# Graph attention layer on one core: row scales turned as 48 columns and spread through memory, with another order of the VectorE work

## The reference

```
q, k = x @ Wq.T, x @ Wk.T            v = x @ Wv.T + bv
scores = q k^T / sqrt(384) + 2*adj          per head, 128 x 128
row_nonzero = any(scores != 0)              per row and head
scores = where(row_nonzero, scores, -inf)
p = nan_to_num(softmax(scores))
out = (p v) @ Wo.T + bo
result = layernorm(x + out)
```

## Time and profile before

| | |
|---|---|
| time, median of 3 runs | 660.97 us (660.78 to 662.17) |
| profiled execution, its own time | 661.33 us |
| its span | 659.5 us |
| busy share of PE, DVE, ACT, POOL | 97%, 76%, 78%, 62% |
| granted clock of TensorE | 0.999 |
| transfers | 45.88 MB, mean 70 GB/s |

### The profile page before, as it was taken

How to read it: one execution, slowest core, us unless ns; L and a number is a source line. 1 busy time by engine, 2 the same in 40 slices (tenths; PEclk the granted TensorE clock), 3 DMA queues, 4 the chain that set the end, 5 groups by cost and what they waited for, 6 DMA issues and landing times.

```text
span 659.5 us, 18322 instructions
## 1 busy us (share of the span) xinstructions
PE 638.3 (97%) x6060; PEld 550.3 (83%) x6060; DVE 502.6 (76%) x2319; ACT 517.6 (78%) x1942; POOL 410.4 (62%) x500
## 2 busy tenths in 40 slices
PE   9999999999999999999999999999999999999774
PEld 5788888888888888888888888888888888888673
DVE  4667887877887777887877887777877877877884
ACT  5678887878878788877878878788877878877782
POOL 1557665756756666765766856666765756845662
PEclk9999999999999999999999999999999999999999
DMA  9300312121121210212121131210212111011111
GB/s 306 122 4 9 106 57 105 57 74 44 48 105 58 104 50 19 95 59 104 58 86 41 38 106 58 104 50 29 85 58 105 57 50 36 32 58 58 49 49 49
DMA packets 17951, 45.88 MB, mean 70 GB/s; under 512 B 1984, under 2 KB 7104, under 8 KB 17856
## 3 DMA queue, kind: packets, MB, share of 16 engines
q1 hardware_dynamic: 17424, 44.11, 19.3%
q10 hardware_dynamic: 432, 0.59, 0.3%
HBM read 32.11 MB, written 12.58 MB: 68 GB/s over the span
## 4 chain that ended last, share of the span: by engine, by line
PE 67%; POOL 16%; issue 8%; DVE 7%; ACT 2%; POOLq 0%
PE qk_ps L279 21%; PE vo_ps L357 11%; POOL tree L230 10%; PE vo_ps L311 10%; PE pt_ps L325 9%; PE scores_ps L296 6%; PE att_ps L342 5%; DVE nscores L498 4%; POOL x_t L212 4%; PE pt_ps L332 2%; ACT probs L409 2%; PE scores_ps L369 1%; PE pt_ps L265 1%; POOL x_n L219 1%; DVE att_t L538 1%
## 5 line engine op out<-in xcount | busy, mean ns | idle before, releaser
L409 ACT ACTIVATE probs<-nscores,neg_max 128x128 f32<-128x128 f32 x768 | 296.7, 391 | 3.1 <-DVE neg_max L498 3.1
L498 DVE CUSTOM_DVE_ANT_0 nscores<-scores_ps,adj_n 128x128 f32<-128x128 f32 x768 | 171.6, 286 | 16.0 <-PE scores_ps L296 16.0
L409 ACT ACTIVATION_READ_ACCUMULATOR probs<-nscores,neg_max 128x1 f32 x768 | 146.5, 191 | 0.0
L230 POOL TENSOR_TENSOR tree<-nscores 128x768 f32<-128x768 f32 x64 | 120.2, 1878 | 36.0 <-DVE neg_max L498 36.0
L325 PE MATMUL pt_ps<-ident,probs 128*128 128x128 f32 x768 | 118.7, 277 | 9.2 <-ACT probs L409 7.0
L357 PE MATMUL vo_ps<-w_o,att_t 128*128 128x384 f32 x576 | 116.8, 347 | 0.0
L212 POOL TENSOR_TENSOR x_t<-x_raw,x_t 128x512 fp32r<-128x512 f32 x45 | 58.4, 1300 | 93.5 <-ACT x_t L426 93.5
L311 PE MATMUL vo_ps<-w_v,x_t 128*128 128x384 f32 x576 | 114.1, 342 | 0.0
L325 PEld LDWEIGHTS pt_ps<-ident,probs 128*128 128x128 f32 x768 | 89.8, 140 | 28.9 <-ACT probs L409 7.9
L230 POOL TENSOR_TENSOR tree<-tree 128x384 f32<-128x384 f32 (+1 forms) x128 | 103.8, 811 | 10.0
L279 PE MATMUL qk_ps<-x_t,w_k 128*128 128x512 f32 x405 | 105.4, 404 | 2.6 <-POOL x_t L212 2.6
(11 more groups left out here) (56 smaller groups left out, 808.2 us busy)
## 6 DMA issues: line engine op xcount, KB each, us to landing
x_n<-xn SPq DMA_DIRECT2D x32, 384.0 KB, 3.6
out<-out_n SPq DMA_DIRECT2D x32, 384.0 KB, 2.6
x_raw<-xt SPq DMA_DIRECT2D x15, 768.0 KB, 5.4
adj_n<-adj SPq DMA_DIRECT2D x32, 128.0 KB, 2.0
x_raw<-xt SPq DMA_DIRECT2D x3, 256.0 KB, 5.5
nscores<-wq ACTq DMA_DIRECT2D x3, 192.0 KB, 4.2
nscores<-wk SPq DMA_DIRECT2D x3, 192.0 KB, 5.5
probs<-wv SPq DMA_DIRECT2D x1, 576.0 KB, 6.4
```

Source lines behind the costliest of these rows:

```text
L230: nc.gpsimd.tensor_tensor(tree[:, b % 2, :, 0:width], src[:, :, 0:width], src[:, :, width:2 * width], ALU.add).then_inc(tree_step, 1)
L409: last = nc.scalar.activation(probs[:, b % 2, h], nscores[:, b % 2, h], ACT.Exp, bias=neg_max[:, b % 2, h:h + 1], scale=-1.0, accum_out=ro ...
L498: last = nc.vector.tensor_tensor_reduce(out=nscores[:, half, h], in0=scores_ps[j][:, m * P:(m + 1) * P], in1=adj_n[:, b // 2 % 2, half], s ...
```

## The change

The row scale is no longer spread over 384 columns before it is turned. DVE writes 48 columns in the order (j, copy, m), where head h = 4m + j and each factor stands in four copies, with three instructions in place of one. PE turns them with one transpose into 48 partitions of `att_ps`, columns 384 to 511. ACT (`keep_rows`) copies these 48 x 128 values to `scale_rows`; SP writes them to memory (48 rows of 512 bytes) and reads them back as 16 rows of 1536 bytes, each into 8 partitions, into `scale_t`. `normalise` waits for that transfer.

The order changes too: `find_scale(b)` stands right behind `bias_and_max(b+1,0)` and ahead of `attention_low(b-1)`; `turn_scale(b)` stands behind the first tile (two-tile iterations) or behind `turn(b,1)`; the copy of the second turned probabilities moves ahead of the third maxima (one-tile iterations) or of the second (no-tile iterations), and in no-tile iterations that part is turned into `qk_ps`. One warm-up matmul at the start is left out. The main parts of the diff:

```diff
+COPIES = DMA // HPT
-        scale_n = sb("scale_n", [P, 2, HID])
+        row_scale = sb("row_scale", [P, 2, HPT, COPIES, KT])
+        scale_rows = sb("scale_rows", [DMA * KT, 2, P])
+        rows_ps = att_ps[0:DMA * KT, HID:HID + P]
+        scale_mem = nc.dram_tensor("scale_mem", (2, DMA, KT * P), F32, kind="Internal").ap()
+        def turned_ps(b, m):
+            return pt_ps if m != 1 or projected(b) else qk_ps[:].rearrange("p (j q) -> p j q", j=HPT)
 # SP, at the head of the loop over b
+                sp.wait_ge(rows_ready, b + 1)
+                sp.dma_start(scale_mem[b % 2].rearrange("c (m q) -> (c m) q", m=KT),
+                             scale_rows[:, b % 2]).then_inc(rows_out, DMA)
+                sp.wait_ge(rows_out, DMA * (b + 1))
+                wait(sp, att_done, b)
+                sp.dma_start(scale_t[:], scale_mem[b % 2].unsqueeze(1).to_broadcast(
+                    [DMA, P // DMA, KT * P])).then_inc(scale_in, DMA)
 # PE
             def turn(b, m):
                 pe.wait_ge(probs_ready, KT * b + m + 1)
                 if m == 0:
-                    wait(pe, scale_t_ready, b)
+                    wait(pe, pt_rest, 2 * b)
+                elif m == 1 and projected(b):
+                    pe.wait_ge(pt_first, b + 1)
                 elif m == 1:
+                    pe.wait_ge(kept, TILES * (NG - 1))
+                elif projected(b):
+                    pe.wait_ge(pt_rest, 2 * b + 1)
+                else:
                     pe.wait_ge(pt_first, b + 1)
-                else:
-                    pe.wait_ge(pt_rest, 2 * b + 1)
 ...
             def turn_scale(b):
                 pe.wait_ge(scale_ready, b + 1)
+                wait(pe, att_split, b)
+                nc.tensor.transpose(rows_ps, row_scale[:, b % 2].rearrange("p j c m -> p (j c m)"),
+                                    ident[:]).then_inc(scale_turned, 1)
+
+            def attend(b):
+                pe.wait_ge(pt_first, b + 1)
                 pe.wait_ge(pt_rest, 2 * b + 2)
-                for m in range(KT):
-                    last = nc.tensor.transpose(pt_ps[:, m], scale_n[:, b % 2, m * P:(m + 1) * P], ident[:])
-                last.then_inc(scale_turned, 1)
-            def attend(b):
                 pe.wait_ge(v_ready, b + 1)
-                wait(pe, att_split, b)
+                pe.wait_ge(rows_ready, b + 1)
 ...
-            run_idle(4)
+            run_idle(3)
 ...
                 if len(tiles) == 2:
                     project(tiles[0])
+                    if has(b):
+                        turn_scale(b)
                 if has(b + 1):
                     values(b + 1)
                 if has(b):
                     turn(b, 1)
+                    if len(tiles) < 2:
+                        turn_scale(b)
                 if tiles:
                     project(tiles[-1])
 ...
                 if has(b):
-                    turn_scale(b)
                     attend(b)
 # ACT: behind softmax_top(b + 1, 0), in place of the copy at L481
+            def keep_rows(b):
+                act.wait_ge(scale_turned, b + 1)
+                wait(act, rows_out, DMA * (b - 1))
+                nc.scalar.activation(scale_rows[:, b % 2], rows_ps, ACT.Copy).then_inc(rows_ready, 1)
 # DVE, find_scale
+                wait(dve, att_high, b)
                 nc.vector.reduce_sum(total, tree[:, half, :, 0:REST], axis=mybir.AxisListType.X).then_inc(total_done, 1)
 ...
-                nc.vector.scalar_tensor_tensor(out=scale_n[:, half].rearrange("p (h d) -> p h d", h=HEADS),
-                                               in0=nonzero.unsqueeze(2).to_broadcast([P, HEADS, D]), scalar=0.0,
-                                               in1=recip[:].unsqueeze(2).to_broadcast([P, HEADS, D]),
-                                               op0=ALU.not_equal, op1=ALU.mult).then_inc(scale_ready, 1)
+                for m in range(KT):
+                    last = nc.vector.scalar_tensor_tensor(
+                        out=row_scale[:, half, :, :, m],
+                        in0=nonzero[:, m * HPT:(m + 1) * HPT].unsqueeze(2).to_broadcast([P, HPT, COPIES]), scalar=0.0,
+                        in1=recip[:, m * HPT:(m + 1) * HPT].unsqueeze(2).to_broadcast([P, HPT, COPIES]),
+                        op0=ALU.not_equal, op1=ALU.mult)
+                last.then_inc(scale_ready, 1)
 # DVE, normalise
-                dve.wait_ge(scale_t_ready, b + 1)
+                dve.wait_ge(scale_in, DMA * (b + 1))
 # DVE, the loop
                 if has(b + 1):
                     bias_and_max(b + 1, 0)
+                if has(b):
+                    find_scale(b)
                 if has(b - 1):
                     attention_low(b - 1)
+                if tiles == 0 and has(b):
+                    keep_turned(b, 1)
                 if has(b + 1):
                     bias_and_max(b + 1, 1)
+                if tiles == 1 and has(b):
+                    keep_turned(b, 1)
+                if tiles and has(b + 1):
                     bias_and_max(b + 1, 2)
+                if has(b + 1):
                     keep_v(b + 1)
-                if has(b):
+                if tiles == 2 and has(b):
                     keep_turned(b, 1)
-                    find_scale(b)
+                if has(b):
                     keep_turned(b, 2)
+                if not tiles and has(b + 1):
+                    bias_and_max(b + 1, 2)
                 if has(b - 1):
                     residual(b - 1)
```

More of the change, by code:

```diff
@@ L130, in build @@
         scale_turned = sem("scale_turned")
-        scale_t_ready = sem("scale_t_ready")
+        rows_ready = sem("rows_ready")
+        rows_out = sem("rows_out")
+        scale_in = sem("scale_in")
         att_done = sem("att_done")
@@ L318, in turn @@
                 if m == 0:
-                    wait(pe, scale_t_ready, b)
+                    wait(pe, pt_rest, 2 * b)
+                elif m == 1 and projected(b):
+                    pe.wait_ge(pt_first, b + 1)
                 elif m == 1:
+                    pe.wait_ge(kept, TILES * (NG - 1))
+                elif projected(b):
+                    pe.wait_ge(pt_rest, 2 * b + 1)
+                else:
                     pe.wait_ge(pt_first, b + 1)
-                else:
-                    pe.wait_ge(pt_rest, 2 * b + 1)
+                dst = turned_ps(b, m)
                 for j in range(HPT):
-                    last = nc.tensor.transpose(pt_ps[:, j], probs[:, b % 2, m * HPT + j], ident[:])
+                    last = nc.tensor.transpose(dst[:, j], probs[:, b % 2, m * HPT + j], ident[:])
                 last.then_inc(turned, 1)
@@ L393, in _ @@
                 if has(b):
-                    turn_scale(b)
                     attend(b)
                 if b == NB - 1:
-                    pe.wait_ge(scale_t_ready, NB)
                     run_idle(2)
@@ L468, in _ @@
                     softmax_top(b + 1, 0)
+                if has(b):
+                    keep_rows(b)
                 if len(tiles) == 2:
@@ L510, in keep_turned @@
                 dve.wait_ge(turned, KT * b + m + 1)
-                nc.vector.tensor_copy(probs_t[:, m * HPT:(m + 1) * HPT], pt_ps[:]).then_inc(pt_rest, 1)
+                nc.vector.tensor_copy(probs_t[:, m * HPT:(m + 1) * HPT], turned_ps(b, m)[:]).then_inc(pt_rest, 1)
             def find_scale(b):
@@ L571, in _ @@
             for b in range(-1, NB + 1):
+                tiles = len(projected(b))
                 if has(b - 1):
@@ L575, in _ @@
                     bias_and_max(b + 1, 0)
+                if has(b):
+                    find_scale(b)
                 if has(b - 1):
                     attention_low(b - 1)
+                if tiles == 0 and has(b):
+                    keep_turned(b, 1)
                 if has(b + 1):
                     bias_and_max(b + 1, 1)
+                if tiles == 1 and has(b):
+                    keep_turned(b, 1)
+                if tiles and has(b + 1):
                     bias_and_max(b + 1, 2)
+                if has(b + 1):
                     keep_v(b + 1)
+                if tiles == 2 and has(b):
+                    keep_turned(b, 1)
                 if has(b):
-                    keep_turned(b, 1)
-                    find_scale(b)
                     keep_turned(b, 2)
+                if not tiles and has(b + 1):
+                    bias_and_max(b + 1, 2)
                 if has(b - 1):
```

## The result

The changed kernel takes 664.28 us in the median (663.98 to 665.58, 5 runs) against 660.97 (5 runs as well): ratio 1.0049, 95% interval 1.0038 to 1.0060, so +3.3 us. The forecast was 662.3, +1.3 by the medians. The profiled execution took 665.58 us, 1.3 above the median, with a span of 663.8 (659.5 before).

The account below looks back on a forecast made before the run. PE bounds 59 iterations, a loop through DVE some five at the end. Iterations +2.4, group starts -1.7, no-tile -0.9, end +1.6 give +1.4 on 661.33: 662.7, or 662.3 us as median; 80% range 653 to 676.

Parts of the forecast that it names:

- the new wait: PE's scale transpose waits for DVE's `find_scale` and `attention_low`; PE stands 0.24 us in one-tile, 0.07 in two-tile iterations.
- B: Start of DVE's first bias operation in an iteration, from which times are counted; 1.02 us behind the first score.
- rival 1: PE's wait for the scale is met almost in time, so PE gains: 655 us, chance 0.30.
- rival 2: DVE's three small products in `find_scale` are dear: 674.7 us at 0.17 each, 670 at 0.14; chance 0.22.
- the single transpose: The scale's one transpose added on PE: 0.10 us per iteration, bounds 0.09 to 0.2.
- what leaves PE: Three scale transposes removed from PE, 0.27 us per iteration; the other 0.14, a change of tile shape before `attend`, stays.
- Everything behind it on PE waits too: PE's stop before the scale's transpose delays all later work and the next B: one-tile iterations +0.07 us, two-tile +0.01.
- That chain changes by about 0.1: Group starts wait for x's last split on POOL, behind ACT: 0.12 us less for each of 14, -1.7 us.
- Transfers: Scale rows' write and read, 4.1 us together, hidden by the rest of the iteration with 1.1 us in hand: cost 0.
- Rival 3: The scale's transfers come late for `normalise` once over 5.1 us together: 735 or 673 us, chance 0.08.
- No-tile iterations: Loop through POOL's tree and DVE: 8.47 us for three against 8.57, the first 7.9; together -0.9 us.
- the end: Last block's `normalise` 16.2 us behind the last B instead of 14.58, nothing left to hide the transfers: +1.6 us.

Follow-up runs that it names:

- experiment 1: Changed kernel with DVE's value-bias addition (`keep_v`) ahead of the third maxima in one-tile iterations: 669.64 us, ratio 1.0120 to the kernel before.
- experiment 3: Changed kernel with the copy of the second turned probabilities back behind the third maxima and `keep_v` in one-tile iterations: 668.53 us, 1.0103 to the kernel before.
- experiment 2: Changed kernel with the scale's two transfers for block 0 alone, all later blocks using that scale: 663.51 us, 1.0031 to the kernel before.
- experiment 7: Changed kernel, in one-tile iterations the scale's transpose behind the projected tile and ACT's row copy behind the second exponentials: 690.92 us, 1.0451 to the kernel before.
- experiment 4: Changed kernel with the scale's transpose of one-tile iterations into free columns of `vo_ps`, not waiting for `attention_low`: 664.74 us, 1.0047 to the kernel before.
- the execution with the fill: Changed kernel with matmuls of zeros in PE's idle time from iteration 59 and before the last block's scale: 663.09 us, 1.0019 to the kernel before.
- the last kernel of experiment 5: Kernel before with the splits of x one iteration sooner and nothing of the change: 655.36 us, ratio 0.9909 to the kernel before.

## Why the forecast was nearly right, step by step

**Right: the new wait.** Forecast release B + 2.53, measured 603.79 - 601.31 = 2.48. PE stands 0.21 us for it in one-tile and 0.05 in two-tile iterations (0.24 and 0.07 forecast), so rival 1 falls. The three small products took 603.09 - 602.84 = 0.25 us, below my 0.30 and its lower bound; rival 2 falls. The overlap of other small operations was the right guide. The 0.43 that follows from the Trainium skill (Perfetto Trace Analysis, Optimizing Scalar/DVE Operations) does not hold for these three; the measurement decides.

**Mis-sized: the single transpose and what leaves PE.** 603.81 - 603.79 = 0.02 us between starts, not 0.10. And 0.32 us left, not 0.27 (in two-tile iterations 0.33): of the 0.14 that I took for a change of shape that stays, only 0.09 stayed. A two-tile iteration is then -0.33 + 0.02 + 0.05 + 0.11 = -0.15, as measured; I had +0.01.

**Failed: "Everything behind it on PE waits too" as the whole price of a one-tile iteration.** The sum has no term for `keep_v`. `find_scale` and the copy, both moved ahead of the third maxima, push its end to B + 5.08 (606.39 - 601.31); PE arrives at B + 5.03 (605.99 + 0.35) and starts at B + 5.23. With measured terms the sum is -0.32 + 0.02 + 0.21 + 0.20 = +0.11, measured +0.12; without the last term it is a gain (experiment 1: 8.65 against 8.71).

**Failed: "That chain changes by about 0.1" (group starts).** A group start was to lose 0.11 (+0.01 - 0.12) and lost 0.07, which looks right and isn't. What it takes over another two-tile iteration was to fall by 0.12 and grew, from 11.26 - 10.80 = 0.46 to 11.19 - 10.65 = 0.54. The split no longer waits for ACT alone: with the third maxima 1.5 us later (they end at B + 3.1 in the earlier trace rows's iteration, at B + 4.6 now) it waits behind POOL's tree. POOL's wait for ACT fell from 93.5 us to 25.7, and its wait for the maxima rose from 36.0 to 101.1. Experiments 1 and 3 move the group starts by +0.65 and -0.54.

**Transfers.** 4.1 us forecast for both, 1.4 + 2.9 = 4.3 measured; hidden, as said, with 1.0 us in hand (1.1 forecast). Rival 3 falls by experiment 2 and its point of decision stands by experiment 7.

**No-tile iterations and the end.** The first took 8.28 where I had 7.9. For the next ones I had 8.47; where the clock held they took 8.50 to 8.53 (experiments 2, 3, 4), and DVE waits for POOL's tree there as forecast (0.38 us in the changed kernel). The clock was in no step. For the end I had +1.6; 28.1 - 25.4 = 2.7 was measured. In the execution with the fill it was 661.5 - 634.24 = 27.3, so +1.9. The 25.4 is not fixed either: in the last kernel of experiment 5, which ends as the kernel before does, the granted clock was 0.78 from 637 to 642, an output projection took 3.06 us in place of 1.83, and the end took 26.9. `normalise` waited for `scale_t` twice:

```profile
637.41 0.57 DVE L567 TENSOR_TENSOR att_ps<-att_ps,scale_t 128x384 f32<-128x384 f32 x1 [1.04 <-DMA scale_t<-scale_mem]
...
653.95 0.57 DVE L567 TENSOR_TENSOR att_ps<-att_ps,scale_t 128x384 f32<-128x384 f32 x1 [1.38 <-DMA scale_t<-scale_mem]
```

The second is the forecast one. The first, 0.29 in place of 1.04 in the execution with the fill, is most of the 0.8 between the two ends: that transfer took 4.4 us to land (median 2.9), for a reason that stays open.

**The start.** Up to the end of iteration 0 the changed kernel is 0.8 us ahead. 0.39 of it is iteration 0, where PE no longer waits for the last copy before it turns the scale. The other 0.38 is the first score's start; whether the missing warm-up matmul does it was not isolated. Over the profiled executions of all kernels with the new path the first score starts at 20.4 to 21.0, at 21.2 and 21.0 with the old one.

**The total.** Being 2.0 us off was luck in part. By the usual lengths, one-tile iterations were forecast at +2.1 us in all and came to +3.6 (30 x 0.12), two-tile ones at +0.3 and came to -4.4 (29 x -0.15), the group starts' own part at -1.7 and came to +1.1 (14 x 0.08), the last iterations and the end at +0.7 and came to +3.6 in the profiled execution. Errors of both signs cancelled.

## What to carry to other kernels

When an order written by hand is changed, list for every instruction that moves back who waits for it, not only for the one that is moved forward: here the moved copy was free and the value copy behind it cost as much as the whole gain. Two waits in a row on one engine hide each other; taking the first away shows nothing, as experiment 4 did, until the second goes too. Work taken from a full engine pays only once its new waits are gone: the same path cost 3.6 us with two stops of 0.2 and gave 6.5 once they were gone but for 0.09. And an end of a few us in which the clock may fall moves a total by 1 to 3 us: compare the iterations, not the totals alone.

## What the runs showed of the chip

PE's granted clock fell from its level of 2.4 GHz towards 1.2 in the last iterations of several executions: nine matmuls took 2.83 us in place of 1.82 after stops of 0.50 and 1.15 us, and 3.13 us in place of 1.85 after 3.13 us of standing still. In the profiled execution of the kernel before it stood at 1.00 there, in that of the same kernel with the splits sooner it fell. In other executions the same stops left it at 1.00.

A transfer of 24 KB to memory landed in 1.4 us (3.0 at most), less than the 2.0 of 128 KB in the other direction, and 192 KB spread from 16 rows took 2.9 (4.4 at most). adj, whose transfer goes out right behind that one, landed in 2.6 us with it and in 2.0 without (experiment 2).

One transpose ahead of a stream of matmuls cost 0.02 us between starts, and the nine matmuls of the values behind it 0.11 more; ahead of other transposes it cost 0.11 (experiment 7). Three DVE instructions of 16 columns with an operand in PSUM took 0.25 us from the first start to the next instruction's.
